# Gates made by GpSimd and stored ahead of two weights; an expert's weights copied ahead of the first rows' normalising

## The chip, the cores and the metric

One Trainium2 chip, one core. The metric is the device time of one execution in microseconds. A core has five engines that run their own instruction streams and meet at semaphores: TensorE (PE), VectorE (DVE), ScalarE (ACT), GpSimd (POOL) and SyncE (SP), and 16 DMA engines that all DMA queues share.

## The reference

The input `x` has 3125 rows of 256. The program is one block of a graph network followed by a mixture of experts:

- rows are normalised; a graph convolution gathers and sums 50,000 weighted edges, `relu([xn, support] @ W + b)`; beside it a hyperbolic linear-attention layer works on the same rows; both are added to `x`;
- then, with `z = layernorm(x)`, a router and eight experts are added:

```
xt      = layernorm(x)
probs   = softmax(xt @ Wr + br);  top 2 of 8, weights = top_p / sum(top_p)
xe      = layernorm(xt) * ln_g[e] + ln_b[e]
h       = gelu(xe @ W1[e] + b1[e])          # 256 -> 1024
y       = h @ W2[e] + b2[e]                 # 1024 -> 256
x      += sum over the two chosen experts of weight * y
```

The kernel computes each token for its two chosen experts alone. The two weights of a token are called its gates here. All matrices are f32.

## The kernel before

The 3125 rows stand in SBUF as `X`, 25 tiles of 125 rows. The first 745 us make the edges, the graph sums and the mixing; they end when VectorE has added everything into `X`. Nothing of that is touched.

**Routing (VectorE, lines 1320 to 1450).** VectorE makes the rows' statistics, TensorE turns each tile and multiplies it by `Wr`, and VectorE takes the two best experts of each row: `oh1`, `oh2` are their one-hot forms (125 x 25 x 8) and `e21` the difference of their logits, of which ScalarE takes the exponential (`row_out` 10). A prefix sum over the tokens gives each of the 6250 (token, expert) pairs a slot, so that the pairs of one expert stand together in blocks of 128; there are at most `TB` = 56 blocks. To turn slots into lists, VectorE builds one-hot columns in five groups (`slot_lists` and `slot_tiles`, lines 1409, 1412, 1418), ScalarE scales them, and TensorE multiplies them (line 711). Between the groups 0 and 1 VectorE makes the gates (`gate_columns`), between 2 and 3 the expert number of each block (`block_experts`, `expert_row`, semaphore `tok_slots`). At the end five small instructions (lines 1446 to 1450) make the indices `fetch` and `home`, and the last one raises `l_idx`.

**SP's queue (lines 360 to 431)** is in an order written out by hand. Near the end: three W2 loads (1 MB each, `load_w2`) beside the graph sums; eight W1 loads (1 MB each) once the sums are through; `X` into `z_d` in HBM, five pieces of two stores, each as its rows are ready; five more W2 loads; a wait for the gates (`g_ready`); two stores of the gates with the rows' scale and bias (10 columns of 40 bytes a row, rows 0 to 111 and 112 to 124 of each tile) behind the rows of `z_d`; then `X` into the output as its base, ten stores.

**GpSimd (lines 438 to 530)** gathers rows for the graph sums until 742 us and then waits for `l_idx`, the stores of the rows (`z_out`) and of the gates (`g_out`). Then it gathers the rows of a block, 128 rows of 266 columns from `z_d`, into one of four buffers `xsb` (line 517), three blocks ahead, and adds each finished block to the output with an indirect store (line 528), the first of these behind the base stores.

**The experts.** For block b VectorE normalises the gathered rows (`normalise`, line 1474), reads the block's expert number (`value_load`, line 1455), copies this expert's W1 (128 x 2048, line 1460), its `ln_g`, `ln_b` and `b1` (lines 1461 to 1463) into fixed places, and scales the turned rows (line 1467, two of 128 x 128, from PSUM). TensorE turns the rows (line 725), multiplies them by W1 (line 735, 32 instructions in the profile's count), and one block later the activated result by W2 (line 746); before the first W2 product it waits until all eight W2 loads are in (`w2_in`). ScalarE applies gelu (line 951) and copies the result out (line 962).

Before the loop, block 0 and the rows of block 1 are prepared in this order on VectorE: `normalise(0, 0)`, which waits for the gathered rows; the wait for W1; `expert_in(0, 0)`; `normalise(1, 0)`.

Of the kernel before, what the change touches and what calls it, by code (L numbers as in the profile page):

```python
# [20 lines left out]
ALU = mybir.AluOpType  # L21
# [9 lines left out]
T = 125  # L31
NT = N // T
# [19 lines left out]
NE, H = 8, 1024  # L52
# [37 lines left out]
def need(eng, sem, count):  # L90

    if isinstance(count, int) and count <= 0:
        return
    eng.wait_ge(sem, count)
# [22 lines left out]
def build(nc, io):  # L117
    with ExitStack() as ctx:
        def sb(name, shape, dt=F32):
            return ctx.enter_context(nc.sbuf_tensor(name, shape, dt))  # L120

        def sem(name):
            return ctx.enter_context(nc.semaphore(name))
# [156 lines left out]
        lg, oh1, oh2, cand, t1, t2 = [cut(200)[0:T, :].rearrange("p (t e) -> p t e", t=NT) for _ in range(6)]  # L280
        cs, pos, logit0 = [cut(200)[0:T, :] for _ in range(3)]
        m1, m2, i1, i2, e21, den1 = [cut(NT)[0:T, :] for _ in range(6)]
# [12 lines left out]
        gates = sb("gates", [128, ZG * NT])[0:T, :].rearrange("p (t e) -> p t e", t=NT)  # L295
# [49 lines left out]
        tok_slots = sem("token_slots_ready")  # L345
        z_out, g_ready, g_out = sem("z_stored"), sem("gates_ready"), sem("gates_stored")
# [3 lines left out]
        xs_in = [sem(f"xs_in{k}") for k in range(4)]  # L350
        m_xt, m_xe, m_g1, m_ge, m_g2, m_y = [sem("m_" + n) for n in ("xt", "xe", "g1", "ge", "g2", "y")]
        m_w1, dve_go = sem("m_w1"), sem("dve_go")
        m_wc, m_xn = sem("m_wc"), sem("m_rows_normalised")
        added = sem("expert_added")

# [3 lines left out]
        def _(sp):  # L359
# [41 lines left out]
            def load_w2(e):  # L401
                sp.dma_start(W2[:, e, :, :], io["W2"][e]).then_inc(w2_in, 16)
# [14 lines left out]
            for u in range(5):  # L417
# [1 line left out]
                sp.wait_ge(n_x, t + 5)  # L419
                sp.dma_start(z_t[0:112, t:t + 5, 0:C], X[0:112, t:t + 5, :]).then_inc(z_out, 16)  # L420
                sp.dma_start(z_t[112:T, t:t + 5, 0:C], X[112:T, t:t + 5, :]).then_inc(z_out, 16)
            for e in (7, 3, 4, 5, 6):
                load_w2(e)
            sp.wait_ge(g_ready, 1)
            sp.dma_start(z_t[0:112, :, C:ZW], gates[0:112, :, :]).then_inc(g_out, 16)
            sp.dma_start(z_t[112:T, :, C:ZW], gates[112:T, :, :]).then_inc(g_out, 16)
            out_t = io["out"][0:N, :].rearrange("(t p) c -> p t c", p=T)
            for u in range(5):
                t = 5 * u
# [4 lines left out]
        def _(pool):  # L434
            P = nc.gpsimd
# [69 lines left out]
            for b in range(EB):  # L505
                need(pool, g_mm, b - GR + 1)
                pool.indirect_dma_start(ring[:, b % GR, :], None, io["y_d"],  # L507
                                        bass.IndirectOffsetOnAxis(gix[:, b:b + 1], 0)).then_inc(gth[b % GR], 16)

            pool.wait_ge(l_idx, 1)  # L510
            pool.wait_ge(z_out, 32 * (NT // 5))
            pool.wait_ge(g_out, 32)
# [454 lines left out]
        def _(v):  # L967
            V = nc.vector
            count = [0]

            def chain(ins):

                count[0] += 1
                ins.then_inc(dve_step, 1)
                v.wait_ge(dve_step, count[0])
# [381 lines left out]
            lift = [T, NT, NE]  # L1357
# [63 lines left out]
            def gate_columns():  # L1421
                v.wait_ge(row_out, 10)
                chain(V.tensor_scalar(den1, e21, 1.0, None, ALU.add))
                chain(V.reciprocal(wgt1, den1))
                chain(V.tensor_tensor(wgt2, wgt1, e21, ALU.mult))
                V.tensor_tensor(t1, oh1, wgt1.unsqueeze(2).to_broadcast(lift), ALU.mult)
                chain(V.tensor_tensor(t2, oh2, wgt2.unsqueeze(2).to_broadcast(lift), ALU.mult))
                V.tensor_tensor(gates[:, :, 0:NE], t1, t2, ALU.add).then_inc(g_ready, 1)

            def block_experts():  # L1430
                chain(V.tensor_tensor(bcmp, iota[0:1, 0:TB].unsqueeze(2).to_broadcast([1, TB, NE]),
# [6 lines left out]
            for g in range(len(LA) - 1):  # L1438
                slot_lists(g)
                slot_tiles(g)  # L1440
                if g == 0:
                    gate_columns()
                if g == 2:
                    block_experts()
# [5 lines left out]
            V.scalar_tensor_tensor(home, lcol, -1.0, ocol, ALU.add, ALU.add).then_inc(l_idx, 1)  # L1450


            def expert_in(b, s):
                h = s % 2
                e = v.value_load(expert_row[0:1, ds(b, 1)], min_val=0, max_val=NE - 1)
                need(v, m_g1, b - 1)
                need(v, m_ge, b - 1)
                need(v, m_xe, 2 * b)
                v.sem_inc(dve_go, 1)
                V.tensor_copy(W1b[h], W1[:, ds(e, 1), :, :].rearrange("p e k h -> p (e k) h")).then_inc(m_w1, 1)  # L1460
                V.tensor_copy(gcol, lng[:, :, ds(e, 1)].rearrange("p k e -> p (k e)")).then_inc(m_gb, 1)
                V.tensor_copy(bcol, lnb[:, :, ds(e, 1)].rearrange("p k e -> p (k e)")).then_inc(m_gb, 1)
                V.tensor_copy(b1c[h], b1T[:, :, ds(e, 1)].rearrange("p k e -> p (k e)")).then_inc(m_gb, 1)
                need(v, m_xt, b + 1)
                need(v, m_gb, 3 * (b + 1))
                for k in range(2):
                    V.tensor_scalar(xeT[h][:, k, :], ps[:, 6, 128 * k:128 * k + 128], gcol[:, k:k + 1],  # L1467
                                    bcol[:, k:k + 1], ALU.mult, ALU.add).then_inc(m_xe, 1)
                need(v, m_y, b - 3)
                V.tensor_copy(wcol[:, s:s + 1], xsb[s][:, C:C + NE][:, ds(e, 1)]).then_inc(m_wc, 1)  # L1470

            def normalise(s, r):
                v.wait_ge(xs_in[s], 16 * (r + 1))
                V.tensor_scalar(xsb[s][:, 0:C], xsb[s][:, 0:C], xsb[s][:, C + NE:C + NE + 1], xsb[s][:, C + NE + 1:ZW],  # L1474
                                ALU.mult, ALU.add).then_inc(m_xn, 1)

            normalise(0, 0)
            v.wait_ge(w1_in, 16 * NE)
            expert_in(0, 0)
            normalise(1, 0)  # L1480

            def expert_v(b, s, r):
                if not isinstance(b, int) or b + 1 < TB:
                    expert_in(b + 1, (s + 1) % 4)
                if not isinstance(b, int) or b + 2 < TB:
                    normalise((s + 2) % 4, r + (s + 2) // 4)
# [34 lines left out]
```

## Time and profile before

| | |
|---|---|
| median of 3 runs | 1257.17 us (1256.51 to 1259.1) |
| profiled execution, its own time | 1254.04 us |
| its span | 1252.2 us |
| TensorE matmul busy | 1028.8 us, 82% |
| VectorE busy | 748.6 us, 60% |
| GpSimd busy | 682.1 us, 54% |
| ScalarE busy | 591.5 us, 47% |
| mean granted TensorE clock | 0.901 |

The span is the time from the first to the last instruction that the profiler saw; the execution's own time holds a little more. In the rows below "us" are microseconds from the start of the span. An instruction's start is when it began on its engine; two instructions of one engine may overlap by some hundredths where the second fills the pipeline behind the first. "SPq", "POOLq" or "DVEq" is the engine's sequencer, which waits on semaphores, issues DMAs and reads registers. A clock of 1.00 is 2.4 GHz for TensorE, 0.50 is 1.2 GHz. "arena_a" to "arena_e", "x", "small", "bn", "node" are the large SBUF tensors from which the kernel cuts its tiles: `xsb` and the routing's tiles lie in arena_e, the lists in arena_d, W1 in arena_a, W2 in arena_c.

### The profile page before, as it was taken

Reading aid. Unit: us, or ns where it says so; the run is one execution under the profiler, and the core shown is the slowest. Engines: PE = TensorE matmul, PEld = TensorE weight load, DVE = VectorE, ACT = ScalarE, POOL = GpSimd, SP = SyncE. Lnnn points to the kernel's source line nnn. Section 1 sums busy time; section 2 is a strip of 40 time slices with the busy share of each in tenths; the row PEclk is TensorE's granted clock in tenths of the full one; section 3 lists DMA queues with packets and bytes.
Section 4 is the critical chain, followed back from the end, with each engine's and each line's share of the span. In section 5 each row is a group of like instructions: output and inputs, shape, how many; then the busy total and the mean of one; then the engine's idle time right before and its main releaser. Section 6 shows DMA issues by size and latency. Waiting matters only on the chain.

```text
span 1252.2 us, 20253 instructions
## 1 busy us (share of the span) xinstructions
PE 1028.8 (82%) x5500; PEld 832.2 (66%) x5501; DVE 748.6 (60%) x1668; ACT 591.5 (47%) x1534; POOL 682.1 (54%) x655
## 2 busy tenths in 40 slices
PE   2399959995778787787877665499999999999996
PEld 1277735553556666566665345389999999999995
DVE  9998846664587777877777788433333333333330
ACT  0154425557777666776676543133333333333331
POOL 4648857777777777777777750123333333333332
PEclk9699969998788888888887777599999999999998
DMA  7012123333333333333333469712222222222221
GB/s 166 0 46 80 35 58 106 106 106 104 102 106 103 104 103 102 103 104 101 102 105 104 137 209 360 237 27 35 34 34 34 34 35 37 36 38 34 34 35 17
DMA packets 57516, 108.12 MB, mean 86 GB/s; under 512 B 16717, under 2 KB 39154, under 8 KB 55394
## 3 DMA queue, kind: packets, MB, share of 16 engines
q0 software_dynamic: 33792, 73.32, 23.5%
q1 hardware_dynamic: 23260, 33.36, 8.6%
q10 hardware_dynamic: 390, 0.60, 0.2%
q8 instruction: 28, 0.46, 0.2%
q14 instruction: 46, 0.38, 0.1%
HBM read 88.83 MB, written 18.40 MB: 86 GB/s over the span
## 4 chain that ended last, share of the span: by engine, by line
PE 57%; DVE 15%; issue 12%; POOL 7%; DMA 4%; ACT 2%; DVEq 2%; ACTq 0%; SPq 0%; POOLq 0%
PE ps L735 16%; PE ps L746 16%; PE ps L605 10%; POOL rec_d L497 6%; PE ps L652 5%; DVE arena_c L1187 4%; PE ps L614 4%; DMA arena_c<-y_d,arena_e 2%; POOL arena_c L507 2%; DMA z_d<-gates 1%; ACT arena_e L827 1%; PE ps L637 1%; PE ps L725 1%; PE ps L568 1%; PE ps L744 1%
## 5 line engine op out<-in xcount | busy, mean ns | idle before, releaser
L507 POOL DMA_INDIRECT arena_c<-y_d,arena_e x440 | 428.9, 975 | 145.0 <-issue 85.9
L605 PE MATMUL ps<-arena_c,arena_e 128*125 128x256 f32 x880 | 270.4, 434 | 112.6 <-DVE arena_c L1187 80.0
L605 PEld LDWEIGHTS ps<-arena_c,arena_e 128*125 128x125 f32 x880 | 169.2, 209 | 192.0 <-issue 138.6
L1187 DVE TENSOR_TENSOR arena_c<-arena_c,ps 125x256 f32 x440 | 183.2, 416 | 104.1 <-PE ps L605 87.2
L528 POOL DMA_INDIRECT out<-arena_a,bn x56 | 91.2, 1629 | 280.9 <-ACT arena_a L962 277.8
L827 ACT ACTIVATE arena_e<-arena_e 128x125 f32<-128x125 bf16 x440 | 201.4, 508 | 83.0 <-PE ps L605 65.6
L746 PE MATMUL ps<-arena_c,arena_d 128*128 x896 | 208.4, 386 | 0.0
L951 ACT ACTIVATE arena_d<-ps,small 128x128 f32<-128x128 f32 x448 | 121.6, 383 | 179.1 <-PE ps L735 179.1
L746 PEld LDWEIGHTS ps<-arena_c,arena_d 128*128 128x128 f32 x896 | 165.6, 190 | 27.0
L1467 DVE TENSOR_SCALAR arena_a<-ps,small 128x128 f32<-128x128 f32 x112 | 40.8, 406 | 173.6 <-PE ps L725 173.5
L735 PEld LDWEIGHTS ps<-arena_a,arena_d 128*128 128x128 f32 x896 | 106.8, 196 | 4.9 <-DVE arena_a L1467 3.5
L735 PE MATMUL ps<-arena_a,arena_d 128*128 128x128 f32 x896 | 107.1, 279 | 3.1 <-DVE arena_a L1467 3.1
L735 PEld LDWEIGHTS ps<-arena_a,arena_e 128*128 128x128 f32 x896 | 104.4, 192 | 2.5 <-DVE arena_a L1467 1.1
L735 PE MATMUL ps<-arena_a,arena_e 128*128 128x128 f32 x896 | 104.7, 275 | 0.8 <-DVE arena_a L1467 0.8
L517 POOL DMA_INDIRECT arena_e<-z_d,bn x56 | 54.9, 979 | 74.0 <-DMA z_d<-gates 57.3
L497 POOL DMA_INDIRECT rec_d<-arena_e x60 | 72.8, 1213 | 32.7 <-issue 17.7
L1237 DVE RECIPROCAL arena_c<-arena_c 125x512 f32<-125x512 f32 x25 | 83.7, 3346 | 2.2 <-issue 2.2
L962 ACT ACTIVATE arena_a<-ps,bn 128x256 f32<-128x256 f32 x56 | 26.5, 474 | 104.8 <-PE ps L746 104.8
L614 PE MATMUL ps<-arena_c,arena_d 128*128 128x500 f32 (+1 forms) x168 | 71.7, 550 | 3.6 <-DVEq L1154 3.6
L652 PE MATMUL ps<-arena_d 128*125 128x256 f32 x200 | 72.4, 527 | 0.0
L652 PEld LDWEIGHTS ps<-arena_d 128*125 128x125 f32 x200 | 57.2, 286 | 15.2
L1474 DVE TENSOR_SCALAR arena_e<-arena_e 128x256 f32<-128x256 f32 x56 | 23.2, 414 | 64.6 <-DMA arena_e<-z_d,bn 64.6
(318 smaller groups left out, 1346.7 us busy)
## 6 DMA issues: line engine op xcount, KB each, us to landing
arena_c<-in_W SPq DMA_DIRECT2D x8, 1024.0 KB
arena_a<-in_W SPq DMA_DIRECT2D x8, 1024.0 KB, 11.8
arena_c<-y_d,arena_e POOLq DMA_INDIRECT x440, 2.8
x<-in_x SPq DMA_DIRECT2D x5, 560.0 KB
z_d<-x SPq DMA_DIRECT2D x5, 560.0 KB
out<-x SPq DMA_DIRECT2D x5, 560.0 KB
y_d<-arena_c SPq DMA_DIRECT2D x15, 125.0 KB
y_d<-arena_a SPq DMA_DIRECT2D x10, 125.0 KB
```

Source lines behind the costliest of these rows:

```text
L497: pool.indirect_dma_start(io["rec_d"], bass.IndirectOffsetOnAxis(didx[0:m, GCOL * k + g:GCOL * k + g + 1], 0), stage[0:m, k, g, :], None). ...
L507: pool.indirect_dma_start(ring[:, b % GR, :], None, io["y_d"], bass.IndirectOffsetOnAxis(gix[:, b:b + 1], 0)).then_inc(gth[b % GR], 16)
L528: pool.indirect_dma_start(io["out"], bass.IndirectOffsetOnAxis(home[:, b:b + 1], 0), ysb[b % 2], None, compute_op=ALU.add, oob_is_err=True ...
L605: nc.tensor.matmul(pair(b), sel[b % SR], ring[:, b % GR, :], start=True, stop=True).then_inc(g_mm, 1)
L614: mm = nc.tensor.matmul(ps[:, j, 0:w], wq[:, k, 128 * j:128 * j + 128], HT[:, k, i * TC:i * TC + w], start=(k == 0), stop=(k == 1))
L652: mm = nc.tensor.matmul(ps[0:T, 5, 0:C], oT[t % 2][:, k, :], wres[:, k, :], start=(k == 0), stop=(k == 3))
L735: mm = nc.tensor.matmul(psf[:, 1024 * s + 128 * j:1024 * s + 128 * j + 128], W1b[s][:, k, 128 * j:128 * j + 128], xeT[s][:, k, :], start=( ...
L746: mm = nc.tensor.matmul(out, gel[s][:, 128 * k:128 * k + 128], W2[:, ds(e, 1), k, :], start=False, stop=(k == 7))
L827: nc.scalar.activation(sel[b % SR], hot[b // 8 % 2][:, :, b % 8], ACT.Copy, scale=wcols[:, b:b + 1]).then_inc(selm, 1)
L951: ins = nc.scalar.activation(gel[s % 2][:, 128 * j:128 * j + 128], psf[:, 1024 * (s % 2) + 128 * j:1024 * (s % 2) + 128 * j + 128], ACT.Ge ...
L1187: V.tensor_tensor(part, part, pair(b), ALU.add).then_inc(g_acc, 1)
L1237: V.reciprocal(rden, den[t % 2]).then_inc(v_at, 1)
```

## The change

Two parts, independent of each other:

1. `gate_columns` on VectorE ends with `wgt2`, which raises a new semaphore `gate_w`. GpSimd waits for it after its last gather for the graph sums, makes the three products and sums (125 x 200 f32, in the scratch tiles `lg` and `cand`), and raises `g_ready`. On SP the wait for the gates and their two stores stand ahead of the W2 loads of experts 5 and 6.
2. For block 0, `expert_in` is entered before the rows are waited for: it reads the expert number and copies W1, `ln_g`, `ln_b` and `b1`, and then calls `normalise(0, 0)`. VectorE waits for `tok_slots` ahead of it.

```diff
-            for e in (7, 3, 4, 5, 6):
+            for e in (7, 3, 4):
                 load_w2(e)
             sp.wait_ge(g_ready, 1)
             sp.dma_start(z_t[0:112, :, C:ZW], gates[0:112, :, :]).then_inc(g_out, 16)
             sp.dma_start(z_t[112:T, :, C:ZW], gates[112:T, :, :]).then_inc(g_out, 16)
+            for e in (5, 6):
+                load_w2(e)
...
+            lift = [T, NT, NE]
+            pool.wait_ge(gate_w, 1)
+            P.tensor_tensor(lg, oh1, wgt1.unsqueeze(2).to_broadcast(lift), ALU.mult)
+            chain(P.tensor_tensor(cand, oh2, wgt2.unsqueeze(2).to_broadcast(lift), ALU.mult))
+            P.tensor_tensor(gates[:, :, 0:NE], lg, cand, ALU.add).then_inc(g_ready, 1)
             pool.wait_ge(l_idx, 1)
...
-                chain(V.tensor_tensor(wgt2, wgt1, e21, ALU.mult))
-                V.tensor_tensor(t1, oh1, wgt1.unsqueeze(2).to_broadcast(lift), ALU.mult)
-                chain(V.tensor_tensor(t2, oh2, wgt2.unsqueeze(2).to_broadcast(lift), ALU.mult))
-                V.tensor_tensor(gates[:, :, 0:NE], t1, t2, ALU.add).then_inc(g_ready, 1)
+                V.tensor_tensor(wgt2, wgt1, e21, ALU.mult).then_inc(gate_w, 1)
...
-            def expert_in(b, s):
+            def expert_in(b, s, first=False):
...
                 V.tensor_copy(b1c[h], b1T[:, :, ds(e, 1)].rearrange("p k e -> p (k e)")).then_inc(m_gb, 1)
+                if first:
+                    normalise(0, 0)
                 need(v, m_xt, b + 1)
...
-            normalise(0, 0)
+            v.wait_ge(tok_slots, 1)
             v.wait_ge(w1_in, 16 * NE)
-            expert_in(0, 0)
+            expert_in(0, 0, first=True)
             normalise(1, 0)
```

## Rows read from the trace of the kernel before

**Rows 1.** The page's first line.

```profile
span 1252.2 us, 20253 instructions
```

**Rows 2.** Chain of waits, 784 to 812: start us, us, what.

```profile
785.85 12.84 DMA z_d<-gates
...
799.46 4.07 DMA arena_e<-z_d,bn
...
803.97 1.09 DVEq L1455
...
807.88 4.21 PE ps L735 x18
```

**Rows 3.** Chain of waits, 690 to 830 and 1225 to 1253.

```profile
819.45 3.65 PE ps L746 x16
...
1228.61 3.57 PE ps L735 x32
```

**Rows 4.** Timeline of VectorE, 782.5 to 795.9: start us, us, what, shapes.

```profile
784.18 0.19 DVE L1425 TENSOR_TENSOR small<-small,arena_e 125x25 f32<-125x25 f32 x1
...
785.08 0.37 DVE L1428 TENSOR_TENSOR gates<-arena_e 125x200 f32<-125x200 f32 x1
785.37 0.95 DVE L1409 TENSOR_TENSOR arena_d<-arena_d 125x1536 bf16<-125x1536 bf16 x1
786.24 0.50 DVE L1412 TENSOR_TENSOR arena_d<-arena_d 125x672 bf16<-125x672 bf16 x1
...
795.55 0.21 DVE L1450 SCALAR_TENSOR_TENSOR bn<-bn 128x56 int32<-128x56 f32 x1
```

**Rows 5.** Timeline of GpSimd, 0 to 110.

```profile
23.00 0.94 POOL L464 TENSOR_TENSOR arena_a<-arena_a,arena_e 125x400 f32<-125x400 f32 x1
...
42.00 3.63 POOL L476 TENSOR_SCALAR arena_c<-arena_d 128x500 f32<-128x500 f32 x1 [16.45 <-DVEq L1053]
...
53.01 2.04 POOL L483 TENSOR_TENSOR arena_d<-arena_d 128x500 f32<-128x500 f32 x1
```

**Rows 6.** Timeline of VectorE, 54 to 59.

```profile
53.12 1.97 DVE L1079 TENSOR_TENSOR small<-small 125x25 f32<-125x25 f32 x1
```

**Rows 7.** Line 1055 by itself: ns min/median/max, first and last start.

```profile
L1055 DVE TENSOR_TENSOR arena_a<-arena_a,arena_e x5: 1187/1194/1597, 42.0 to 46.8; 125x2000 f16<-125x2000 bf16 x5
```

**Rows 8.** Timeline of SP's queue, 640 to 830.

```profile
774.04 3.41 SPq L402 DMA_DIRECT2D arena_c<-in_W  x5
...
785.85 8.26 SPq L426 DMA_DIRECT2D z_d<-gates  x1
```

**Rows 9.** Windows: us, busy of each engine, PEclk, DMA share, GB/s.

```profile
745.00:746.00 1.00, 0.00 (x0) 0.00 (x0) 0.86 (x3) 0.00 (x0) 0.00 (x0) 1.00 0.38 49
...
782.00:790.00 8.00, 3.26 (x29) 2.83 (x30) 7.73 (x17) 2.56 (x3) 0.00 (x0) 0.50 1.01 424
...
793.00:794.00 1.00, 0.99 (x10) 1.00 (x11) 0.36 (x2) 0.48 (x1) 0.00 (x0) 0.50 0.12 12
```

**Rows 10.** Gathers' issue to landing: line 517 (795 to 806), line 507 (733 to 739).

```profile
DMA to landing us min/median/max: 4.1/5.9/6.6
...
DMA to landing us min/median/max: 2.7/5.0/5.9
```

**Rows 11.** Timeline of VectorE, 750 to 822.

```profile
803.56 0.41 DVE L1474 TENSOR_SCALAR arena_e<-arena_e 128x256 f32<-128x256 f32 x1 [7.79 <-DMA arena_e<-z_d,bn]
...
806.82 0.17 DVE L1463 COPY small<-small 128x8 f32 x1
807.10 0.73 DVE L1467 TENSOR_SCALAR arena_a<-ps,small 128x128 f32<-128x128 f32 x2
```

**Rows 12.** Timeline of TensorE, 795 to 850.

```profile
804.12 0.66 PE L725 MATMUL ps<-small,arena_e 128*128 128x128 f32 x2 [9.49 <-DVE arena_e L1474]
```

**Rows 13.** Windows of the two starts of TensorE.

```profile
808.00:813.00 5.00, 5.00 (x24) 5.00 (x25) 1.62 (x5) 0.35 (x1) 0.00 (x0) 0.50 0.01 3
...
765.00:769.00 4.00, 3.99 (x22) 3.95 (x23) 3.35 (x18) 1.25 (x5) 0.00 (x0) 0.57 1.00 329
```

More of the change, by code:

```diff
@@ L352, in build @@
         m_w1, dve_go = sem("m_w1"), sem("dve_go")
+        gate_w = sem("gate_weights_ready")
         m_wc, m_xn = sem("m_wc"), sem("m_rows_normalised")
```

## The prediction, made before the change was run

> **What bounds the kernel now.** I read the span first [rows 1], then the chain of waits around the change [rows 2], then the end of the chain [rows 3]. The reader is to see two regimes. From 807.88 us on the chain is TensorE alone: 56 expert blocks, 3.65 us of second-layer and 3.57 us of first-layer products in each, with nothing waited for. So whatever moves the start of the first block's products moves the end by as much, and nothing later can give it back. Before 807.88 the chain runs through the making of the gates on VectorE, their store by SP (12.84 us from issue to landing), the first gather of token rows by GpSimd (4.07 us), and then VectorE; TensorE only waits for them. Both edits lie on this stretch. The question is how much earlier the 807.88 comes.
>
> **Part 1: gates made by GpSimd.** VectorE had wgt2 at 784.37 and then made three products and sums, ending at 785.45; its next list product started at 785.37 [rows 4]. Without them that product starts at about 784.40, so VectorE's list work moves up by 0.97 us. This work is followed back to back until the indices l_idx, whose last instruction ended at 795.76 [rows 4]: 794.8 if nothing else changes.
> GpSimd needs three TENSOR_TENSOR of 200 f32 elements. The nearest row is one of 400 elements, 0.94 us [rows 5]; half of that is 0.47, and with a fixed part I take 0.57, so 1.7 us for three. Undisturbed: 784.5 + 1.7 = 786.2. But GpSimd and VectorE disturb each other in this trace. A TENSOR_SCALAR of 500 elements took 3.63 us beside VectorE's 125x2000 products, three times as much an element as the 0.94 us row; and VectorE's 25-element product took 1.97 us beside a GpSimd product of 2.04 us that had begun 0.11 us ahead, while VectorE's five 2000-element products had 1.19 us as median and 1.60 at most [rows 5 to 7]. So the one that starts first is finished first. In the new place VectorE runs a 0.95 us product and two of about 0.50 us, again and again without a gap [rows 4], so each GpSimd instruction may wait for one of them, in all up to 2.0 us: gates ready between 786.2 and 788.2; I take 787.5, since the first one meets the 0.95 us product already running. In return VectorE is held by each GpSimd instruction for 0 to 0.57 us: l_idx between 794.8 and 796.5; I take 795.4, as the nearest row (0.4 us lost once by the 2000-element products, 1.60 against 1.19) says that VectorE loses little.
> The Trainium skill, page "SBUF — State Buffer", section "Who interferes with whom", says that a VectorE instruction with two SBUF inputs and a GpSimd instruction that reads SBUF exclude one another, whoever starts first keeping the shared ports for its whole instruction. By that rule every list product collides; l_idx would be at 796.5 and come last, and the time 1253.4, inside the forecast's own range below. The rows agree for the short product, and less clearly for the five long ones.
>
> **Part 2: the store ahead of two weights.** SP issued five W2 loads from 774.04 to 777.45 and then stood waiting for the gates [rows 8]; so the three that stay ahead are issued by then in the new kernel too, and SP waits for the gates with nothing else behind it that is due. What changes is what lies in the rings ahead of the gates. In 782 to 790 the DMA engines moved 424 GB/s and were full; in 793 to 794 there were 12 GB/s, small gate packets [rows 9]. The loads' backlog thus ended at about 791.5, and the gates landed at 785.85 + 12.84 = 798.69 [rows 2]: 7.2 us of their own behind the backlog (two stores, the second held by SP until 794.11 [rows 8]). Two loads of 1.05 MB at 424 GB/s are 4.9 us; without them the backlog ends at 786.6. That is before the gates are ready, so the store now waits for GpSimd, not for the rings: gates at 787.5, plus 0.40 for the first issue (785.45 to 785.85 [rows 2, 4]), plus a start-up of at most 1 us (the first W1 load, issued at 744.86, already shows 0.38 of DMA share in 745 to 746 [rows 9]; I take 0.4), plus 7.2, is 795.5. Bounds: if the descriptors need no more than half of the 7.2, and the gates are ready at 786.2, 791; if some engine stays as late as before, 798.7, no gain at all.
> The gather waits for the later of l_idx and this landing: 795.4 and 795.5. GpSimd started 0.77 us after the landing [rows 2], so the first gather goes from 799.46 to 796.3: 3.2 us earlier. Even with the gates at 791 it could not start before 794.8 + 0.77 = 795.6, which is 3.9 us earlier at most.
>
> **The gather itself** took 4.07 us beside the base stores [rows 2]; the four gathers there took 4.1 to 6.6 us to land, and five others beside a single 1 MB load 2.7 to 5.9 [rows 10]. In the new kernel the two weights are issued behind the gates, near 791.5 to 792, and need 5 us, until about 797.5, so they overlap the beginning of the gather; the base stores follow as before. I take 4.8 us (between 4.1 and 5.9), 0.7 lost. First rows in SBUF: 801.1 instead of 803.53, 2.4 us earlier.
> The Trainium skill, page "DMA: Bandwidth & Descriptors", section "Queues, rings and completion order", says that an engine alternates between its queues packet by packet. By it a gather shares time even with a long queue rather than waiting for the end of it; a FIFO over both queues would have the gather wait for all that is ahead, 1 to 2 us here. The gathers beside a 1 MB load [rows 10] agree: at 5.9 us at most none waited for several loads.
>
> **Part 3: the expert's weights ahead of the normalising.** Before, everything was behind the rows: normalising at 803.56, reading of the expert number from 803.97, copies until 806.99, then the two scalings of 128x128, and TensorE at 807.88 [rows 2, 11]: 4.35 us after the rows landed. The number and copies cost 806.99 - 803.97 = 3.0 us. Now VectorE starts them after its last list instruction (795.4 + 3.0 = 798.4) and is done before the rows land at 801.1; that wait for the rows is the cover, and it has 2.7 us of slack. The W1 loads that they read are long in SBUF: 8.4 MB at 424 GB/s from 745.4 end near 765. Behind the rows remain: normalising and the step to TensorE 0.56 (803.56 to 804.12), two transposes 0.66, two scalings 0.73 and two semaphore steps of 0.05 [rows 11, 12]: 2.1 us with the first step of 0.03. Gain 4.35 - 2.1 = 2.25 us. If the rows landed at once with l_idx, the copies would be exposed by up to what they overtake; the gather's 4.1 us forbids that. The b1 and gamma copies that release ScalarE's table load (1.28 us) are also earlier; that load is hidden before and after.
>
> **The sum.** Start of the first products: gather start -3.2, gather +0.7, order -2.25, together -4.75 us. Two loads fewer ahead of the gates also means two loads later for TensorE's wait for all of W2, which stands before its first second-layer product (819.45 [rows 3], 814.7 in the new kernel); at 5 us after 792 they are there. Block 2's and 3's gathers are needed only after the first block's 6 us. The first products ran at a granted clock of 0.50 (1.2 GHz) from 807.88 until 813.0 or so [rows 13], as TensorE had mostly idled before: 5.1 us at half speed. When the token transposes set in at 765, the mean of 0.57 over 4 us says that 3.4 us were slow [rows 13]. So the slow stretch will be there again, and may differ by 1.7 us; at half speed that is 0.9 us of work either way.
> The profiled execution has 1254.04 us with a span of 1252.2; it lies 3.1 us below the median of the runs. Own time 1254.0 - 4.75 = 1249.3; by the median 1257.17 - 4.75 = 1252.4 us. A change under 0.2%, 2.5 us, is about what a measurement of this kernel can't tell from none.
>
> **Rivals.**
> A smaller gain: the store doesn't come earlier. For it: 3125 packets of 40 bytes have 7.2 us by themselves, GpSimd's gates come 2 us later than VectorE's did, and any slow engine delays the landing; against it: the low traffic in 793 to 794 shows that the rings were not the limit there, and that time starts when the backlog ends. The gather then starts at 799 and only part 3 is left: 1257.2 - 2.3 = 1254.9.
> A larger gain: l_idx at 794.8, gates landed by then, gather 4.1 us, the clock's rise early: -3.9 - 2.25 - 0.9 = -7.0, 1250.2.
> Slower: the two weights of 1 MB are now issued last of the weights, just ahead of 3.2 MB of base stores, and TensorE waits for all 128 counts of W2 before its first second-layer product. Issued at 792 and landing after 814.7 + 4.75 = 819.5, which takes 27.5 us, they would lose what the rest gains; each us beyond is one us slower. Place: between the second block's first-layer products and its predecessor's second layer; at 30 us it would be 1257.2 + 2.5 = 1259.7. Against it: the rings keep their order, and the whole traffic until then is 2.1 + 0.1 MB, 5 us.
> The change does not do what it says: the gates' later readiness (GpSimd's start after long idling, or VectorE holding it through all of the lists until 793.4) puts the store behind 793.5 instead of 787.5: landing near 801.5, gather 2.8 later, against 2.25 won: 1257.7.
>
> **How the numbers follow.** Forecast -4.75: 0.62, with its own range 1250.5 to 1254.7 (the gates' 791 to 797, the gather's 4.1 to 5.9, the clock's 0.9). Smaller gain 0.20; larger 0.09; slower by W2 0.02; gates late 0.07. The range for 8 in 10 reaches to the larger gain and takes in the smaller one and the measured spread (1256.51 to 1259.1, about 1.3 each way): 1249.3 to 1256.8. Faster by over 0.2%: 0.62 x 0.93 + 0.20 x 0.45 + 0.09 = 0.76, slower: 0.02 + 0.03 = 0.05, rest 0.19.
>
> **What would show it.** Right: three GpSimd products near 784.5 to 788; the store issued right after; the gates landed near 795.5; the first gather's start near 796.3 with l_idx within 1 us of it; the weights' copy on VectorE done at about 798.4 and idle until the rows; 2.1 us from rows to the first-layer products, at 803.1; from there the same 7.65 us a block. Wrong: gates landing at 798 or later; copies that end after the rows; a wait of TensorE before line 746's first product in the changed kernel; a slow clock longer than 6 us; or list products stretched by over 1.7 us in all.

## The result, and the profile after

| | before | changed |
|---|---|---|
| median of 5 runs each | 1257.17 us (1253.61 to 1259.1) | 1252.07 us (1251.39 to 1253.36) |
| ratio | | 0.9967 (95%: 0.9953 to 0.9980) |
| profiled execution, own time / span | 1254.04 / 1252.2 us | 1252.07 / 1250.3 us |

The change makes the kernel 0.33% faster (0.2 to 0.47%). In a later comparison on a chip that runs this kernel in 1371 us it was 0.998 (0.9965 to 0.9996). The two medians differ by 5.1 us, which is more than the change's own stage moved (2.9 us, below), because the stage of the graph sums ahead of it scatters by over 4 us: the end of wgt2 (the second gate weight of each token), which the change does not touch, fell at 784.37 us before and at 785.30 in the changed kernel's profile, and on chips of this speed up to 788.86 in the others. **So from here on, times are counted from the end of wgt2 (+0).** That works even between chips: those that needed 110 us more spent them ahead of that point.

The chain of waits of the changed kernel around the change (start us, us, what), which answers to [rows 2]:

```profile
787.40 0.76 POOL gates L517
...
788.55 8.00 DMA z_d<-gates
...
797.32 7.40 DMA arena_e<-z_d,bn
...
806.79 5.27 PE ps L743 x30
```

The gates landed at 796.54 (+11.25, before +14.32), and the gather started 3.07 us earlier (+12.02 against +15.09). But it took 7.40 us where it had taken 4.07, so the rows were in SBUF 0.26 us later than before (+19.42 against +19.16). From rows to products it was 2.07 us where it had been 4.35; TensorE's first product is at +21.49 instead of +23.51. GpSimd's timeline shows its three products, and that the first gather's instruction (line 525) took twice the 0.94 us of the kernel before:

```profile
785.39 1.18 POOL L515 TENSOR_TENSOR arena_e<-arena_e,small 125x200 f32<-125x200 f32 x1 [42.23 <-DVE small L1433]
786.53 0.79 POOL L516 TENSOR_TENSOR arena_e<-arena_e,small 125x200 f32<-125x200 f32 x1
787.40 0.75 POOL L517 TENSOR_TENSOR gates<-arena_e 125x200 f32<-125x200 f32 x1
797.32 1.91 POOL L525 DMA_INDIRECT arena_e<-z_d,bn  x1 [9.17 <-DVE bn L1455]
```

VectorE's timeline, answering to [rows 4, 11]: three list products are stretched beside GpSimd's (0.85, 0.72 and 1.36 us against 0.50, 0.51 and 0.95, together 0.97 us), the index instruction (line 1455) ends at +11.28, and the copy of W1 (line 1465) runs just when GpSimd begins the gather:

```profile
785.22 0.95 DVE L1417 TENSOR_TENSOR arena_d<-arena_d 125x1536 bf16<-125x1536 bf16 x1
786.08 0.85 DVE L1420 TENSOR_TENSOR arena_d<-arena_d 125x672 bf16<-125x672 bf16 x1
786.96 0.72 DVE L1426 TENSOR_TENSOR arena_d<-arena_d 125x672 bf16<-125x672 bf16 x1
787.61 1.36 DVE L1417 TENSOR_TENSOR arena_d<-arena_d 125x1536 bf16<-125x1536 bf16 x1
...
796.37 0.21 DVE L1455 SCALAR_TENSOR_TENSOR bn<-bn 128x56 int32<-128x56 f32 x1
797.14 1.23 DVE L1465 COPY arena_d<-arena_a 128x2048 f32 x1 [0.56 <-issue]
```

Windows of the changed kernel (us, busy of each engine, PEclk, DMA share, GB/s), answering to [rows 9]:

```profile
792.00:797.00 5.00, 1.62 (x14) 1.39 (x14) 3.14 (x11) 1.33 (x2) 0.00 (x0) 0.50 0.94 104
797.00:805.00 8.00, 0.00 (x0) 0.00 (x0) 1.70 (x5) 1.28 (x1) 4.75 (x4) 0.50 1.00 367
```

Nearly all gate packets had gone out by 792. For the next 5 us the two loads behind them kept the DMA engines 94% busy and moved only 104 GB/s. The prediction had them through at 797.5 (+13.1); in the trace the last of them landed at +18.4, a microsecond before the gather's rows.

### The profile page after: what moved, and what is told of

The parts are those of the page before. It is cut to its first block, busy times and chain, and to the rows that moved or that the text cites. A ratio compares the mean times of both kernels' runs of the same rounds, so it can differ in the third digit from the quotient of the medians.

```text
span 1250.3 us, 20254 instructions
## 1 busy us (share of the span) xinstructions
PE 1030.2 (82%) x5500; PEld 832.8 (67%) x5501; DVE 748.8 (60%) x1665; ACT 592.3 (47%) x1534; POOL 686.2 (55%) x658
## 4 chain that ended last, share of the span: by engine, by line
PE 58%; DVE 15%; issue 12%; POOL 7%; DMA 4%; DVEq 2%; ACT 2%; SPq 0%; ACTq 0%; POOLq 0%
PE ps L743 16%; PE ps L754 16%; PE ps L613 10%; POOL rec_d L500 6%; PE ps L660 5%; PE ps L622 5%; DVE arena_c L1195 5%; DMA arena_c<-y_d,arena_e 2%; PE ps L645 1%; PE ps L733 1%; PE ps L576 1%; DVEq L1183 1%; PE ps L752 1%; ACT arena_e L835 1%; PE ps L638 1%
## 5 line engine op out<-in xcount | busy, mean ns | idle before, releaser
L591 PEld LDWEIGHTS ps<-arena_a 125*128 125x128 bf16 x400 | 54.2, 147 | 10.5 <-issue 10.5
## 6 DMA issues: line engine op xcount, KB each, us to landing
arena_a<-in_W SPq DMA_DIRECT2D x8, 1024.0 KB, 12.6
```

## The experiments

All times in this table are from the profile of each kernel, in us from the end of wgt2. "Instr." is the first gather's instruction on GpSimd, "gather" is from its start to its landing.

| kernel | start | instr. | gather | rows in | first product | end of span | ratio to before (95%) |
|---|---|---|---|---|---|---|---|
| before | 15.09 | 0.94 | 4.07 | 19.16 | 23.51 | 467.84 | |
| changed | 12.02 | 1.91 | 7.40 | 19.42 | 21.49 | 464.97 | 0.9967 (0.9953 to 0.9980) |
| e11, changed again | 12.07 | 1.84 | 6.65 | 18.72 | 20.78 | 464.34 | 0.9980 (0.9965 to 0.9996) |
| e1, part 1 alone | 11.87 | 0.98 | 5.66 | 17.53 | 21.49 | 465.21 | 0.9989 (0.9973 to 1.0004) |
| e2, part 2 alone | 14.99 | 0.94 | 4.90 | 19.89 | 21.96 | 465.33 | 0.9982 (0.9965 to 0.9999) |
| e3, gates on VectorE | 11.66 | 1.64 | 6.55 | 18.21 | 20.28 | 464.09 | 0.9979 (0.9957 to 1.0001) |
| e5, copy on ScalarE | 11.91 | 0.98 | 5.67 | 17.58 | 19.64 | 464.22 | 0.9978 (0.9965 to 0.9991) |
| e7, base stores held | 12.15 | 1.78 | 4.93 | 17.07 | 19.14 | 462.95 | 0.9967 (0.9954 to 0.9981) |
| e4, loads and base held | 11.54 | 1.63 | 3.42 | 14.96 | 17.03 | 461.13 | 0.9959 (0.9936 to 0.9982) |
| e9, before, base held | 12.56 | 0.95 | 2.76 | 15.31 | 18.48 | 462.62 | 0.9971 (0.9958 to 0.9984) |
| e10, e2 with base held | 13.42 | 0.95 | 2.75 | 16.17 | 18.24 | 461.75 | 0.9977 (0.9962 to 0.9992) |
| e6, e4 and e5 together | 11.54 | 0.98 | 2.78 | 14.31 | 16.38 | 460.90 | 0.9953 (0.9938 to 0.9969) |
| e12, e6 again | 11.55 | 0.98 | 2.76 | 14.31 | 16.37 | 460.93 | 0.9933 (0.9915 to 0.9950) |
| e8, e6, gates on VectorE | 11.67 | 0.94 | 2.75 | 14.42 | 16.48 | 460.63 | 0.9936 (0.9918 to 0.9954) |

e1 to e4 ran on a chip on which the kernel before took 1367 us, e8, e10, e11 and e12 on one with 1371 us, e5 to e7 and e9 on one with 1257.5 us. The ratios tell some of these kernels apart, not all; where they do not, what is said below rests on the stage's times alone, that is on one profile of each kernel. The changed kernel and e6 were profiled twice.

**e1: part 1 alone.** What differs from the changed kernel:

```diff
-            v.wait_ge(tok_slots, 1)
+            normalise(0, 0)
             v.wait_ge(w1_in, 16 * NE)
-            expert_in(0, 0, first=True)
+            expert_in(0, 0)
```

> Part 1 alone: gates by GpSimd and stored ahead of W2 of experts 5 and 6, but the rows normalised ahead of the copies as before. Times counted from the end of wgt2. What is to be told apart is why the first gather took 7.40 us in the changed kernel against 4.07 before. Theory A (two causes): VectorE's 1.23 us copy of W1 held GpSimd while it wrote the gather's descriptors (its instruction took 1.91 us, not 0.94), and the queued weights and base stores cost the rest. Here no copy runs then: the gather's instruction takes 0.95 us and the gather 6.2 to 6.6 us. Theory B (the traffic alone): 7.2 to 7.6 us, and the instruction may still take 1.9 us, as the first one after long idling. Either way the gather starts 3 us earlier than before, from rows to the first products stay 4.35 us, and the first products start 0.7 us earlier (A) or 0.2 us later (B) than before, so the time is within 0.1% of before.

The instruction took 0.98 us and the gather 5.66, so the copy is part of the cause (A). The gather is shorter than A's 6.2 to 6.6: against the changed kernel's first profile (7.40) the copy cost 1.7 us, more than A gave it, against its second one (6.65, e11) 1.0. The traffic alone, at 5.66 against 4.07, still costs 1.6. The products start as early as in the changed kernel's first profile (+21.49): rows to products are 3.96 here, so part 2, added to part 1, won 1.89 us behind the rows and lost the same 1.89 ahead of them. Against e11 it lost 1.19.

**e2: part 2 alone.**

```diff
-            for e in (7, 3, 4):
+            for e in (7, 3, 4, 5, 6):
...
-            for e in (5, 6):
-                load_w2(e)
...
-            P.tensor_tensor(gates[:, :, 0:NE], lg, cand, ALU.add).then_inc(g_ready, 1)
+                V.tensor_tensor(gates[:, :, 0:NE], t1, t2, ALU.add).then_inc(g_ready, 1)
```

> Part 2 alone: gates by VectorE and stored behind all five loads as before; only the copies go ahead of the first rows. The copy is then through (about 3 us after the list indices) before the gates land, so it meets no gather: the gather's instruction 0.95 us, the gather 4.1 us, from rows to products 2.07 us instead of 4.35. Start of the products 2.3 us earlier, time 2.3 us less (0.998). If it is 4 us less, the store's move brought nothing at all in the changed kernel.

The order's gain is as expected, 2.07 instead of 4.35; the copy ended ahead of the gather and the instruction took 0.94. The gather itself took 4.90 rather than 4.07, on another chip but with nothing changed around it, so 0.8 us between two loaded gathers may be scatter, as the 0.75 between the changed kernel and e11 is. The first products are 1.55 us earlier, not the 2.3 expected.

**e3: the changed kernel with the gates made by VectorE.**

```diff
-            P.tensor_tensor(gates[:, :, 0:NE], lg, cand, ALU.add).then_inc(g_ready, 1)
+                V.tensor_tensor(gates[:, :, 0:NE], t1, t2, ALU.add).then_inc(g_ready, 1)
```

> The changed kernel, but with the gates made by VectorE as before (no GpSimd products), store still ahead of the two loads, copies ahead. From the end of wgt2: gates ready at 1.1 us instead of 2.85, landing about 1.5 us earlier than in the changed kernel; the list products are not held (0.50, 0.51, 0.95 us) but start 1 us later, so the indices come at 11.4 us, as in both. The gather waits for the indices, at 12.1: same time as the changed kernel within 0.1%. That is, making them on GpSimd wins nothing since its holding of VectorE eats the 1 us. The rival: GpSimd's products were what freed VectorE, and this one is 1 us slower.

The indices come at +11.39 against +11.28, as expected. GpSimd's gates win nothing for VectorE: what it is spared (0.97 us) it loses by being held (0.97 us), and the gates are ready 1.8 us later. The gather starts at +11.66, not at the 12.1 expected, and ahead of the changed kernel's +12.02 and +12.07. Here it follows the indices by 0.27 us, since the gates landed at +9.3; in the changed kernel it waits for the gates' landing at +11.25. In that queue, making the gates on GpSimd delayed the start by 0.4 us.

**e4: a quiet gather.**

```diff
+            sp.wait_ge(xs_in[0], 16)
             for e in (5, 6):
                 load_w2(e)
```

> The changed kernel, but SP holds W2 of 5 and 6 and the base stores until the first gather has landed, so the DMA engines are free for it. Theory A: its instruction still takes 1.9 us beside the copy, the gather 3.9 to 4.1 us (2.9 unloaded plus 1.0), 3.4 us less than 7.40, and the time 3 us less than the changed kernel's unless the loads then arrive late (needed 10 us later). Theory B': the copy alone costs the 3.3 us by keeping descriptors from being written: the gather stays at 6 to 7 us.

The gather took 3.42 us. B' is out; the instruction, at 1.63 us, is still stretched beside the copy, as A says, but the gather is shorter than A's 3.9 to 4.1, so the copy costs less here than A's 1.0 us (0.64, see e6). The gather also starts 0.5 us earlier than in the changed kernel, since the gates landed at +10.1, without loads behind them. The loads are not late: TensorE did not wait at its first W2 product.

**e5: the copy of block 0 on ScalarE.** ScalarE waits for the lists and W1, reads the expert number and copies; VectorE passes the semaphore on.

```diff
+            e0 = act.value_load(expert_row[0:1, 0:1], min_val=0, max_val=NE - 1)
+            nc.scalar.activation(W1b[0], W1[:, ds(e0, 1), :, :]..., ACT.Copy).then_inc(w1_copied, 1)
...
+                if first:
+                    v.wait_ge(w1_copied, 1)
+                    v.sem_inc(m_w1, 1)
+                else:
-                V.tensor_copy(W1b[h], ...).then_inc(m_w1, 1)
+                    V.tensor_copy(W1b[h], ...).then_inc(m_w1, 1)
```

> The changed kernel, but W1 of block 0 is copied by ScalarE instead of VectorE; everything else stays. It isolates the collision of VectorE's copy with the first gather's instruction. Theory A (the copy holds GpSimd): the gather's instruction takes 0.95 us instead of 1.91, and the gather 5.6 us, as with the store alone (5.65), instead of 7.40 or 6.55; rows to products stay 2.1 us; the first products 1 to 1.7 us earlier than in the changed kernel. Rival (the first gather instruction is slow after GpSimd's other work, or the traffic alone varies): the instruction stays at 1.6 to 1.9 us and the gather at 6.5 to 7.4 us.

A again: the instruction is back at 0.98 us and the gather at 5.67, as in e1, and the products start 1.1 to 1.9 us ahead of the changed kernel's. The rival, an instruction slow after long idling or by the traffic, is out. GpSimd's and ScalarE's timelines of e5: the gather's instruction beside ScalarE's copy is not stretched.

```profile
800.07 0.98 POOL L526 DMA_INDIRECT arena_e<-z_d,bn  x1 [9.06 <-DVE bn L1462]
```

```profile
799.26 1.91 ACT L959 ACTIVATE arena_d<-arena_a 128x2048 f32 x1 [1.99 <-PE ps L720]
```

e9 below shows the same collision at another place, where the copy meets the fourth gather instead of the first. VectorE's and GpSimd's timelines of e9:

```profile
805.00 1.23 DVE L1461 COPY arena_d<-arena_a 128x2048 f32 x1 [0.39 <-issue]
```

```profile
803.92 0.94 POOL L518 DMA_INDIRECT arena_e<-z_d,bn  x1 [0.30 <-issue]
805.17 1.88 POOL L518 DMA_INDIRECT arena_e<-z_d,bn  x1 [0.30 <-issue]
```

The Trainium skill, page "SBUF — State Buffer", section "SBUF: two separate sides", states this: while VectorE copies in a two-port mode, GpSimd cannot write the descriptors of its DMAs. The traces agree, with 1.63 to 1.91 us where the two meet and 0.94 to 0.98 where they do not; no row names the copy's mode. They also show which part of the instruction is held. Where the copy had begun first (changed, e11, e7, e9), the instruction ended 0.8 to 0.9 us after the copy, that is nearly its whole length. Where the instruction had begun 0.3 us ahead of it (e3, e4), it ended 0.12 us after the copy.

**e7: only the base stores held.**

```diff
+            sp.wait_ge(xs_in[0], 16)
             out_t = io["out"][0:N, :].rearrange("(t p) c -> p t c", p=T)
```

> The changed kernel, but only the base stores wait for the first gather; W2 of 5 and 6 go out at once as in the changed kernel. It tells which of the two transfers costs the first gather its time. Theory W (the two loads with their 8 KB packets): they need 5 us from about 6 us after wgt2, so they end near 11.5, when the gather starts; if their tail matters the gather takes 5 us or more. Theory S (the base stores, which had started ahead of the gather in every kernel so far): 3.4 us as with both held, and the first products near 17.0.

4.93 us, which is near W's 5 and not S's 3.4: against 3.42 with both held the loads cost 1.5 us, and the base stores 1.7 to 2.5 more (6.65 and 7.40). Both transfers cost the gather time.

**e9: the kernel before, base stores held.**

```diff
             sp.dma_start(z_t[112:T, :, C:ZW], gates[112:T, :, :]).then_inc(g_out, 16)
+            sp.wait_ge(xs_in[0], 16)
             out_t = io["out"][0:N, :].rearrange("(t p) c -> p t c", p=T)
```

> The kernel before, with one edit: the base stores wait until the first gather has landed. Before, they went out 4.6 us ahead of the gather, which then took 4.07 us (4.90 in the kernel with the copies alone). Without them: gather 2.8 us, first products 1.3 to 2.1 us earlier than before, the gates' landing 0 to 0.5 us earlier too (the stores shared the engines with the last gate packets). Rival: stores of 1 KB packets cost a gather nothing, and 4.07 stays.

The gather took 2.76 as expected. Not expected was the other half: the gates landed at +11.78 instead of +14.32 (0 to 0.5 us was expected), though the base stores stand behind them on the queue. So the products start 5.0 us earlier than before, not 1.3 to 2.1. The chain of waits of e9:

```profile
790.33 10.31 DMA z_d<-gates
...
801.41 2.76 DMA arena_e<-z_d,bn
```

Against 12.84 and 4.07 in [rows 2]. With one added wait, the old kernel's products start at +18.48, 2.3 to 3.0 us ahead of the changed kernel's; most of what part 1 was to win by its order (a gather that starts 3.1 us earlier) was had here (2.5 us) with the gates left behind all five loads.

**e6: quiet gather and ScalarE's copy together.** The edits of e4 and e5:

```diff
+            sp.wait_ge(xs_in[0], 16)
             for e in (5, 6):
                 load_w2(e)
...
+            nc.scalar.activation(W1b[0], W1[:, ds(e0, 1), :, :]..., ACT.Copy).then_inc(w1_copied, 1)
```

> Both costs taken away: W1 of block 0 copied by ScalarE, and W2 of 5 and 6 and the base stores held back until the first gather has landed. Theory A: instruction 0.95 us, gather 2.7 to 2.8 us against 3.42 with the hold alone; rows to products 2.1 us unless ScalarE's copy (some 2 us from the end of the list products) is later than the rows, which would show as a wait on it; first products at 16.3 us after the end of wgt2 against 17.0 with the hold alone, 21.5 changed and 23.5 before. Time 6 to 7 us less than before. Rival: if the copy cost nothing in the quiet case, 17.0 as with the hold alone.

As expected to 0.1 us. Windows of e6 over the gather, against 1.00 and 367 GB/s above:

```profile
799.50:802.30 2.80, 0.00 (x0) 0.00 (x0) 0.51 (x3) 1.94 (x2) 2.16 (x3) 0.50 0.18 49
```

**e10: the kernel before with copies ahead and base held.** Against the kernel before:

```diff
+            sp.wait_ge(xs_in[0], 16)
             out_t = io["out"][0:N, :].rearrange("(t p) c -> p t c", p=T)
...
-            normalise(0, 0)
+            v.wait_ge(tok_slots, 1)
             v.wait_ge(w1_in, 16 * NE)
-            expert_in(0, 0)
+            expert_in(0, 0, first=True)
```

> The kernel before with two edits only: base stores held until the first gather has landed, and the copies of block 0 ahead of its rows. Gates stay on VectorE and behind all five loads. If the base stores were what delayed both the gates' landing (14.3 us after wgt2 before, 11.8 with the stores held) and the gather, this needs none of part 1: gates landed at 11.8, gather starts at 12.6, instruction 0.95 to 1.9 us (the copy now runs from 12.9, beside it), gather 2.8 to 3.7, rows to products 2.1: first products at 17.4 to 18.3 us after wgt2, against 21.5 changed and 18.5 with the hold alone. Rival: the loads ahead of the gates matter as part 1 supposes, then products come after 19.

The gates landed at +12.65 and the gather started at +13.42, both 0.9 us later than e9's, on which the expectation of 11.8 and 12.6 was built; why is not shown. There was no collision, since the copy ended at +13.17. The products start at +18.24, in the range expected. Neither of part 1's edits is in it, and it is 2.5 to 3.3 us ahead of the changed kernel in this stage, though its ratio cannot tell them apart.

**e8: e6 with VectorE's gates.** Against e6:

```diff
-            P.tensor_tensor(gates[:, :, 0:NE], lg, cand, ALU.add).then_inc(g_ready, 1)
+                V.tensor_tensor(gates[:, :, 0:NE], t1, t2, ALU.add).then_inc(g_ready, 1)
```

> As the quiet kernel with ScalarE's copy, but the gates made by VectorE as before. GpSimd's products held the list products by 0.97 us, just what VectorE was spared; so the indices come at 11.4 instead of 11.27 us after wgt2, the gather starts at 11.7, takes 2.8, and the products start at 16.5 against 16.4: the same time. If moving the gates to GpSimd had a value, this is 1 us slower.

16.48, as expected: with the loads and stores held, it does not matter where the gates are made (0.1 us).

**e11 and e12: the changed kernel and e6 once more, on one chip.**

> The changed kernel itself once more, beside the others on one chip. Its first gather took 7.40 us once; with the same structure and VectorE's gates 6.55. If the gather's time scatters with the state of the queues, it takes 6 to 8 us here; instruction 1.6 to 1.9 us; first products 20 to 22 us after wgt2 (before 23.5); time 3 to 5 us less than before.

> The quiet kernel with ScalarE's copy again, as the candidate for the best version, on the same chip as the changed one: first products at 16.4 us after wgt2, 5 us ahead of the changed kernel's 21.5; time 4 to 6 us less than the changed kernel's and 7 us less than before.

The changed kernel's gather scatters (6.65 after 7.40), e6's does not (2.76 after 2.78). e11's products start at +20.78, inside its expectation, but it is 2.7 us faster than before (3 to 5 expected). e12 is among the two best versions (e8 measures the same): its products start 4.4 us ahead of e11's, the span ends 3.4 us sooner after wgt2, and the intervals to the kernel before, 0.9915 to 0.9950 and 0.9965 to 0.9996, lie apart. The chain of waits of e12 has no transfer of gates in it, only the indices:

```profile
913.65 0.04 DVE bn L1462
...
914.24 2.76 DMA arena_e<-z_d,bn
...
919.06 5.95 PE ps L745 x27
```

## Why the prediction was right, and which term of it was not

The forecast was 1252.4 us and faster; measured 1252.07. The mechanism stands, but one term, the gather's, was wrong by 1.9 to 2.6 us of a forecast gain of 4.75, and the sum met the median also because an earlier stage scatters and the slow stretch was shorter. That the number fits is luck to this extent.

- **Gates on GpSimd.** Forecast ready at 3.1 us after wgt2, measured 2.85. VectorE's loss was taken as 0.6 us and was 0.97 (three stretched products), so the indices were at +11.28, not +11.0. The rule of the Trainium skill that the prediction set against the rows (page "SBUF — State Buffer", section "Who interferes with whom") has each GpSimd product collide with a list product, and in the trace each of the three stretched one. But 0.97 us were lost in all, nearer to the forecast's 0.6 than to the 1.7 that the prediction made of the rule, which would have put the indices at +12.1.
- **The store ahead of two loads.** Landing forecast at +11.1, measured +11.25 and +11.29; start of the gather forecast at +11.9, measured +12.02 and +12.07. That it fits is luck: the 7.2 us of the gates' own time was carried over from a landing that the base stores had delayed (e9, 2.5 us), and the delay by the two loads now behind the gates was put at nothing. Without those loads the gates land at +10.1 (e4, e6) and +9.8 (e12), 1.1 to 1.5 us earlier than in the changed kernel, and the gather then starts at +11.54, right behind the indices.
- **The gather itself: the wrong term.** "I take 4.8 us ..., 0.7 lost": it took 7.40 and 6.65, so 2.6 to 3.3 us were lost. Two causes were shown. First, the loads were taken to need 5 us at 424 GB/s and to be over at 797.5; they moved 104 GB/s for their first 5 us and ran into the gather together with the base stores. In the five profiles with both in the queues (changed, e11, e1, e3, e5) the gather's first packet went out 3.0 to 3.3 us after the end of its instruction, in the quiet ones (e4, e6, e9, e12) after 0.7. The prediction held that a gather shares time with a long queue, against a FIFO that would cost 1 to 2 us; an added wait of 2.3 to 2.6 us is there, though in e7 the gather's packets ran beside those of the loads, after 1.2 us. Which order the queues follow is left open. Unloaded, a gather takes 2.76; under loads and stores without a collision 5.66 and 5.67 (e1, e5). Second, part 3 placed a 1.23 us copy beside the gather's instruction, which costs 0.64 us in the quiet case (3.42 against 2.78) and 0.9 to 1.7 in the loaded one. The prediction named the wait for the rows as the cover of the copies, and asked only whether the copies end in time, not what GpSimd does meanwhile. So the two parts do not add: first products 2.02 us earlier by part 1, 1.55 by part 2, 2.02 and 2.73 by both.
- **The order.** Forecast 2.25 us, measured 4.35 to 2.07: 2.28. It is worth that much only under load: without part 2, rows to products are 3.96 in e1 and 3.17 in e9, so that the order would win 1.1 there. The difference is in the first reading of the expert number, whose piece of 1.09 us in [rows 2] is 0.70 in e1 and missing in e9; why it is longer while transfers run was not tested.
- **The sum.** Forecast 4.75 at the first product; the traces have 2.02 and 2.73, and 2.9 and 3.5 at the end of the span, as the first block's slow stretch was shorter (32 products in 5.50 us against 6.26), which the prediction had left open at 0.9 us. Its granted clock rose 3.5 us after the first product, where it had been 5.1 (windows below); in e11 it was 4.3 and in e12 5.6, which accounts for 0.7 of the 1.0 us by which e12's lead over e11 has shrunk at the end (4.4 to 3.4). The ratio 0.9967 is 4.1 us (2.5 to 5.9), and 0.998 on the other chip 2.7. The median's 5.1 us contain scatter of the earlier stage, so that it agreed with 4.75 is partly luck.
- **The rivals.** The slower case by the wait for W2 did not come up: no kernel here waited at its first W2 product, not even where the loads went out at +14.3. The smaller gain of 2.3 us came close in size, by another way: not since the store was late but since the gather took back what the store had won.

Windows of the slow part of the first 32 products, before and changed:

```profile
807.88:812.99 5.11, 5.11 (x24) 5.11 (x25) 1.74 (x6) 0.47 (x1) 0.00 (x0) 0.50 0.01 5
```

```profile
806.79:810.29 3.50, 3.50 (x16) 3.50 (x17) 1.77 (x6) 0.00 (x0) 0.00 (x0) 0.50 1.07 372
```

## What to carry to other kernels

When a store or a load is moved ahead so that a gather can start sooner, ask what is in the queues when the gather runs: here holding back transfers that were not due yet started the first products 3.7 to 4.5 us earlier (e4), more than either part of the change. When work is moved into an engine's idle time, list what the other engines do in that time: here a VectorE copy beside GpSimd's gather delayed the gather, and ScalarE's copy did not. Compare profiles from a point that the change cannot reach.

## What was not expected of the hardware

- Two 1 MB loads right behind the 3125 gate packets of 40 bytes moved 104 GB/s for 5 us with the DMA engines busy throughout; loads into the same tensor moved 424 GB/s in [rows 9]. Issued behind the gather instead (e4, e6, e12) they no longer delay the first one. Their 8 KB packets took 1.1 to 1.3 us each on average, where those of [rows 9] took 0.31. They were back near 0.31 from about +12 on, when the gates had landed (+11.25), and from +10 in e3, where the gates landed at +9.3; the two go together in these profiles, but why they are slow there was not settled.
- Stores queued behind the gates' stores delayed their landing: +14.32 and, without them, +11.78 and +12.65. In the changed order, with loads between, it made no difference (11.25 and 11.29 against 11.37 in e7). This was not followed further.
- Chips of one kind differed by 110 us on this kernel, and everything after wgt2 agreed to within 1 us.
